# A causal attention loop of sixteen groups, its steps put in another order on every engine

## The reference, cut to what matters

```python
x = x + _L0_xattn_ref(_layernorm(x), ctx, Wq, Wk, Wv, ..., causal mask)
q, k, v = (xn @ W).reshape(B, T, H, hd).transpose(0, 2, 1, 3)
attn = einsum('bhqd,bhkd->bhqk', q, k) * scale
kernels = softmax(...).reshape(B * H, 1, 3, 3)      # one 3x3 kernel for each head, from ctx
attn = conv3x3(where(mask, 0, attn), kernels)       # over (query, key)
p = softmax(where(mask, -inf, attn))
out = einsum('bhqk,bhkd->bhqd', p, v); return out @ proj_W + proj_b
```

## Time and profile before

| | us |
|---|---|
| median of 3 runs | 1688.47 (1685.16 to 1690.96) |
| profiled execution, time | 1679.27 |
| its span | 1677.5 |
| TensorE busy in the span | 1115.9 (67%) |
| VectorE busy | 1040.9 (62%) |
| GpSimd busy | 586.5 (35%) |
| ScalarE busy | 524.2 (31%) |

### The profile page before, as it was taken

One profiled execution on the slowest core, in us unless ns is written; L12 is line 12 of the kernel. 1 busy time (PEld: TensorE's weight loads), 2 busy tenths in 40 slices (PEclk: granted clock), 3 DMA queues, 4 the chain that ended last, 5 costly groups with the idle time before them and its releaser, 6 DMA issues. The chain is left out here.

```text
span 1677.5 us, 25997 instructions
## 1 busy us (share of the span) xinstructions
PE 1115.9 (67%) x9324; PEld 732.0 (44%) x9324; DVE 1040.9 (62%) x2987; ACT 524.2 (31%) x1045; POOL 586.5 (35%) x680
## 2 busy tenths in 40 slices
PE   1466988887838992565555289877857987866520
PEld 0333434443325991565545278633326962322210
DVE  2465676766632344799999646465534436578897
ACT  0123444343413551222222033224513522433310
POOL 7042323223241453111031544311244541166675
PEclk8578989898859995555555589889967988876665
DMA  4910000000013222543341012240001220022232
GB/s 118 335 46 1 1 1 1 1 1 14 4 47 103 69 62 73 140 119 99 98 124 47 32 56 65 71 125 1 13 26 50 74 74 13 1 78 82 84 101 83
DMA packets 74245, 106.19 MB, mean 63 GB/s; under 512 B 11501, under 2 KB 55712, under 8 KB 71616
## 3 DMA queue, kind: packets, MB, share of 16 engines
q1 hardware_dynamic: 59968, 72.16, 15.4%
q0 software_dynamic: 14144, 32.32, 6.3%
HBM read 77.10 MB, written 27.33 MB: 62 GB/s over the span
## 5 line engine op out<-in xcount | busy, mean ns | idle before, releaser
L833 POOL DMA_INDIRECT y_d<-arena,goal x138 | 132.5, 960 | 187.9 <-DVE arena L916 114.1
L1682 DVE CUSTOM_DVE_ANT_0 arena<-ps,far 128x512 f32<-128x512 f32 (+3 forms) x256 | 116.5, 488 | 63.2 <-PE ps L1374 61.9
L2015 POOL DMA_INDIRECT wide<-in_w_ud,arena x128 | 130.1, 1017 | 68.5 <-issue 36.4
L2935 PE MATMUL ps<-wide,arena 78*128 78x32 bf16 x3840 | 109.9, 187 | 50.1 <-ACT wide L3048 41.6
L2935 PEld LDWEIGHTS ps<-wide,arena 78*128 78x128 bf16 x3840 | 109.1, 104 | 56.3 <-ACT wide L3048 45.5
L1012 PEld LDWEIGHTS ps<-arena 128*128 128x128 f32 (+1 forms) x1012 | 123.2, 191 | 4.1
L1012 PE MATMUL ps<-arena 128*128 128x128 f32 (+1 forms) x1012 | 123.6, 274 | 0.0
L1291 POOL TENSOR_SCALAR_AFFINE_SELECT arena<-arena 128x520 f32<-128x520 f32 (+1 forms) x64 | 41.1, 653 | 159.8 <-ACT arena L1557 159.7
L1374 PE MATMUL ps<-fr 32*128 32x256 f32 (+3 forms) x256 | 82.9, 402 | 18.4 <-DVE arena L1682 16.7
L1557 ACT ACTIVATE arena<-ps 128x1024 f32<-128x1024 f32 x80 | 78.4, 1022 | 50.8 <-PE ps L1395 50.8
L1003 PE MATMUL ps<-arena 128*128 128x256 f32 x368 | 89.3, 386 | 1.6 <-DVE arena L892 1.6
(11 more groups left out here) (514 smaller groups left out, 2606.0 us busy)
## 6 DMA issues: line engine op xcount, KB each, us to landing
arena<-low_d SPq DMA_DIRECT2D x32, 780.0 KB
xs_d<-zrow SPq DMA_DIRECT2D x1, 10320.0 KB, 36.0
arena<-xs_d SPq DMA_DIRECT2D x69, 129.0 KB, 2.1
arena<-y_d SPq DMA_DIRECT2D x16, 256.0 KB, 3.2
arena<-in_w SPq DMA_DIRECT2D x2, 1408.0 KB, 9.0
y_d<-arena,goal POOLq DMA_INDIRECT x138, 2.2
wide<-in_Wfc SPq DMA_DIRECT2D x1, 2048.0 KB, 11.5
wide<-in_Wproj SPq DMA_DIRECT2D x8, 256.0 KB, 6.7
```

Source lines behind the costliest of these rows:

```text
L833: pool.indirect_dma_start(out=y_d, in_=yb[:, i % 2, c, :], in_offset=None, out_offset=bass.IndirectOffsetOnAxis(ap=goal[:, i % 4, c:c + 1] ...
L1682: ins = nc.vector.tensor_tensor_reduce(junk[:, n % 2, 384 * i:384 * i + w], ps[:, n % 2, 384 * i:384 * i + w], far[:, T - w:T], 1.0, 3 * N ...
L2015: pool.indirect_dma_start(out=rows_g[t % 4][:, h, :], out_offset=None, in_=A["w_ud"], in_offset=bass.IndirectOffsetOnAxis(ap=eidi[:, t % 8 ...
L2935: mm = nc.tensor.matmul(ps[:, 2 * (i % 3) + h // 2, col:col + 4 * HD], ring[m_ % 4][:, h * NK + p_, t % 2 * P:t % 2 * P + P], table[n // 4 ...
```

## The change

The same instructions are issued with the exception of the join, which is cut in two; what changes is their order.

- **TensorE**: a group begins with `scores(G, 0)`, then `top(0)`. The three query matmuls stand one by one between `top(0)` and `top(3)`. The other steps are dealt out between the tops anew; `weighted(3G+2)` moves from the next group to the end of its own, behind `maximum_rows(G+1)`, and `shifted(.., 2)`, `normed` and the router's turn stand ahead of `maximum_rows`. `projected`, `logits` and `places` stand behind it.
- **VectorE**: `near_scores` of a key group, `near_shift` and the router's `norms` are at the head of the next group; then ten maxima, `outputs`, two maxima, `maximum_out`. `mixed_keys` is cut: its first two passes (`first_mix`) stand between `maximum_out` and `maximum_in`, its third (`last_mix`) behind `maximum_in`. `join` does heads 0 to 11 at the end of the fourth group of an item and heads 12 to 15 at the end of the next group; both stand behind `maximum_in`.
- **ScalarE**: `keys_rounded` is last in a group, `queries` is behind the first exps, `near_exps` ahead of the third.
- **GpSimd**: `products` is behind the third `select`.
- The list of uses of bank 7 follows.

```diff
@@ TensorE
+                        scores(G, 0)
                         top(0)
-                        if G + 2 <= last:
-                            queries(G + 2)
-                        top(1)
-                        scores(G, 0)
-                        top(2)
-                        if G:
-                            weighted(3 * G - 1)
-                        top(3)
+                        for dy in range(3):
+                            if G + 2 <= last:
+                                queries(G + 2, dy, dy + 1)
+                            top(dy + 1)
+
+                        scores(G, 1)
+                        top(4)
+                        weighted(3 * G)
+                        top(5)
                         if G + 2 <= last:
                             keys(G + 2)
...
+                        top(6)
+
+                        scores(G, 2)
+                        top(7)
+                        if nb < B:
+                            shifted(nb, nt, 0)
+                        top(8)
+                        weighted(3 * G + 1)
+                        top(9)
+                        if G:
+                            outputs_turned(G - 1)
+                        top(10)
+                        if nb < B:
+                            shifted(nb, nt, 1)
+                        top(11)
                         if G % 4 == 1 and G >= 5:
                             joined(G // 4 - 1)
...
                         if nb < B:
                             shifted(nb, nt, 2)
                         if G % 4 == 2 and G // 4 + 2 < B:
                             normed(G // 4 + 2)
                         if G % 4 == 3 and G >= 7:
                             R_.turn(pe, take, G // 4 - 1)
+                        if G + 1 <= last:
+                            maximum_rows(G + 1)
+                            weighted(3 * G + 2)
+                        if G % 4 == 1 and G >= 5:
+                            projected(G // 4 - 1)
@@ VectorE
                     for G in range(G4):
+                        nb, nt = near_key(G - 1)
+                        if G and nb < B:
+                            near_scores(nb, nt)
+                        if G % 4 == 3:
+                            near_shift(G // 4)
+                        if G % 4 == 2 and G >= 6:
+                            R_.norms(dve, G // 4 - 1)
                         if G + 1 <= last:
-                            maxima(G + 1, 0, 6)
-                        if G + 2 <= last:
-                            mixed_keys(G + 2)
-                        if G + 1 <= last:
-                            maxima(G + 1, 6, 9)
+                            maxima(G + 1, 0, 10)
                         if G:
                             outputs(G - 1)
                         if G + 1 <= last:
-                            maxima(G + 1, 9, 12)
+                            maxima(G + 1, 10, 12)
                             maximum_out(G + 1)
...
-                        if G % 4 == 0 and G:
-                            join(G // 4 - 1)
+                        if G + 2 <= last:
+                            first_mix(G + 2)
+                        if G + 1 <= last:
+                            maximum_in(G + 1)
+                        if G + 2 <= last:
+                            last_mix(G + 2)
                         if G % 4 == 1 and G >= 5:
                             projected(G // 4 - 1)
...
+                        if G % 4 == 3:
+                            join(G // 4, 0, 3 * H // 4)
+                        if G % 4 == 0 and G:
+                            join(G // 4 - 1, 3 * H // 4, H)
+                        if G % 4 == 0 and G // 4 + 2 < B:
+                            norms(G // 4 + 2)
+                        if G % 4 == 1 and G // 4 + 2 < B:
+                            normed(G // 4 + 2)
+                        if G % 4 == 1 and G >= 9:
+                            R_.pick(dve, ch, G // 4 - 2)
                         if G % 4 == 2 and G >= 6:
                             R_.normed(dve, G // 4 - 1)
...
                     outputs(last)
                     R_.take_logits(dve, ch, arrived, 2)
-                    join(B - 1)
+                    join(B - 1, 3 * H // 4, H)
@@ GpSimd
                         to_experts(1)
+                        to_experts(2)
                         if G % 4 == 2 and G >= 6:
                             R_.rstd_of(pool, ch, G // 4 - 1)
+                        select(3 * G + 2)
+                        to_experts(3)
                         if nb < B:
                             products(nb, nt)
-                        to_experts(2)
-                        select(3 * G + 2)
-                        to_experts(3)
```

More of the change, by code:

```diff
@@ L1203, in first_causal @@
                     plan("q", G + 2); plan("k", G + 2)
-                if G % 4 == 1 and G >= 5:
-                    plan("num", G // 4 - 1)
                 if nb < B:
@@ L1341, in normed, with queries @@
                         mm.then_inc(turn7, 1)
-                    def queries(G):
-                        take("q", G)
-                        pe.wait_ge(free7_act, emptied(place7["ln", G // 4])[0])
-                        for dy in range(3):
+                    def queries(G, lo=0, hi=3):
+                        if lo == 0:
+                            take("q", G)
+                            pe.wait_ge(free7_act, emptied(place7["ln", G // 4])[0])
+                        for dy in range(lo, hi):
                             mm = nc.tensor.matmul(bnk(7), wq_rows[:, G % 4, dy, :], xnp[:, G // 4 % 2, 1 + dy:1 + dy + T],
                                                   start=dy == 0, stop=dy == 2)
-                        mm.then_inc(turn7, 1)
+                        if hi == 3:
+                            mm.then_inc(turn7, 1)
                     def keys(G):
@@ L1462, in _ @@
+                        top(8)
[4 more added lines that the diff above has]
+                        top(10)
+                        if nb < B:
+                            shifted(nb, nt, 1)
+                        top(11)
                         if G % 4 == 1 and G >= 5:
                             joined(G // 4 - 1)
-                        top(6)
-                        if nb < B:
-                            shifted(nb, nt, 0)
@@ L1467, in _ @@
-                        top(7)
-                        weighted(3 * G)
-                        top(8)
-                        if G:
-                            outputs_turned(G - 1)
-                        top(9)
-                        scores(G, 2)
-                        if nb < B:
-                            shifted(nb, nt, 1)
-                        top(10)
-                        weighted(3 * G + 1)
-                        top(11)
                         if nb < B:
                             shifted(nb, nt, 2)
-                        if G % 4 == 1 and G >= 5:
-                            projected(G // 4 - 1)
@@ L1491, in _ @@
                             R_.places(pe, take, G // 4 - 2)
-                        if G + 1 <= last:
-                            maximum_rows(G + 1)
                     weighted(3 * last + 2)
@@ L1597, in _ @@
                         if G + 2 <= last:
+                            queries(G + 2)
+                        exps(G, 1)
+                        if G + 2 <= last:
                             keys(G + 2)
-                        exps(G, 1)
+                        if G % 4 == 3:
+                            near_exps(G // 4)
+                        exps(G, 2)
+                        if nb < B:
+                            shifted(nb, nt, 0)
+                            shifted(nb, nt, 1)
                         if G % 4 == 1 and G >= 5:
@@ L1603, in _ @@
                         if nb < B:
-                            shifted(nb, nt, 0)
-                        if G + 2 <= last:
-                            keys_rounded(G + 2)
-                        exps(G, 2)
-                        if nb < B:
-                            shifted(nb, nt, 1)
                             shifted(nb, nt, 2)
@@ L1646, in mixed_keys, with first_mix @@
                     def mixed_keys(G):
+                        first_mix(G)
+                        last_mix(G)
+                    def first_mix(G):
                         dve.wait_ge(free7_act, emptied(place7["k", G])[0])
@@ L1730, in projected @@
+                        ins = nc.vector.tensor_tensor(four(num), four(num), wide(dn), ALU.mult)
+                        if hi == H:
+                            ins.then_inc(c["num"], 1)
                     def projected(b):
@@ L1781, in _ @@
                             R_.slots(dve, ch, arrived, G // 4 - 2)
-                        if G + 1 <= last:
-                            maximum_in(G + 1)
-                        if nb < B:
-                            near_scores(nb, nt)
+                        if G % 4 == 3:
+                            join(G // 4, 0, 3 * H // 4)
```

(7 more changed lines are left out.)

54 lines of the change are left out of this document (25 added, 29 removed).

## The result

The changed kernel takes 1725.64 us (median of 4 runs, 1723.83 to 1727.17), the kernel before on the same chip 1686.82 (1683.61 to 1690.96): ratio 1.0222, 95% interval 1.0189 to 1.0255. It is 38.8 us slower; 14.2 were forecast, and the range ended at 1717.

A forecast was written before the change was run, and what follows sets the result against it. The loop was taken as paced by TensorE plus its idle time. Full-clock loop +21 us, less about 4 for the clock and 2.5 in the tail, gave +14.2: 1688.5 + 14.2 = 1702.7 us, range 1681 to 1717.

The forecast's parts named there:

- the term for the clock: Loop time lost to TensorE work at 1.2 GHz: 19 us against 23.35 before, so about 4 us given back.
- my third rival: Short gaps around `maximum_rows` put half of all groups at the low clock: another 12 us, 1715; chance 0.18.
- The path at the full clock: Loop of groups 0 to 14 if always at 2.4 GHz: 309 us against 288.1 before, +21.
- The stalls S: Waits of `top(2)` at the head of each group for VectorE's first maxima: 30 us in all.
- The closing chain T and the contention: From `top(11)`'s end to `maximum_in`'s end, 55.4 us over 15 groups; VectorE and GpSimd hindering each other make about 7.
- TensorE's own work W: TensorE's work up to the end of `top(11)`: 15.4 us in an ordinary group, 217 in all.
- H: From the end of `maximum_in` to `scores(G, 0)`: 0.05 us, 1.1 to 1.2 in five groups, 6.5 in all.
- Group 3: Sign in the profile after: this ordinary group of the loop takes 19 to 20 us, not 17.1.
- Group 12: Sign in the profile after: this group, which had a whole join, gets shorter by 3 to 5 us.
- The tail: Behind the last outputs the join is only 4 heads, 2.2 us for 4.75: -2.5 us.
- Slower still: Rival: short gaps in every group bring the low clock to half of all groups, another 12 us, 1715; chance 0.18.
- The spreading works: Rival: the 5 to 6 us idle times in the closing chain and their low-clock stretches go: -12, 1676; chance 0.16.

The follow-up runs named there:

- b_qsplit: The kernel before with only its three query matmuls dealt out behind tops 0, 1 and 2; ratio 1.0264 to the kernel before.
- a_fill: The changed kernel with spare full-width matmuls, their results unread, where TensorE stands idle; ratio 1.0064 to the kernel before.
- a_qblock: The changed kernel with the three query matmuls in one block behind the first top; ratio 1.0087 to the kernel before.
- b_join_gaps: The kernel before with the join dealt out in small steps between the maxima; ratio 1.0069 to the kernel before.

## Why the prediction was wrong

**The step that failed is the term for the clock**: "I take eight stretches with about 4.2 us of work in each and the one at the start as it is, 19 us lost against 23.35". It measured 46.6 us, in fourteen stretches with 6.65 us of work each, the one at the start among them with 11.59 us and not 4.42. Both factors were too low. The number: I let the clock fall only at idle times of 2 to 5 us, though my third rival said that most low stretches of the kernel before belonged to shorter ones; ahead of the 13.70 us in group 13 no idle time was longer than 1.25 us. The length: a stretch can last 13.7 us with TensorE never idle, where I had taken it to end once the work was dense again. That b_qsplit and a_fill move the loss both ways with VectorE's list untouched shows that it follows the order and the make-up of TensorE's work.

**The path at the full clock was right**: 305.5 us against 309, in part by luck, as the terms show (cut in after's trace as the forecast cut them, half of the low-clock work taken off):
- *The stalls S*: the ten waits ahead of the third top come to 27.2 us, forecast 30. Group 4 had 4.84 (forecast 4.9), group 5 4.22 (3.4), group 8 3.82 (4.9), group 10 2.79 (2.9), group 12 none (1.1).
- *The closing chain T and the contention*: T comes to 54.6 us over the loop, forecast 55.4; group 3 takes 3.51 us from the last top to the end of `maximum_in`, forecast 3.15 to 3.65. Each of the two three-operand steps of the mix is slowed where `products` runs, as the lines view over the loop shows (busy us, mean ns, idle before); at 752 ns the 28 of them would take 6.3 us less, and the forecast had some 7:

```profile
L1660 DVE SCALAR_TENSOR_TENSOR arena<-arena,wcol 128x512 f32<-128x512 f32 x14 | 14.2, 1014 | 0.5
...
L1665 DVE SCALAR_TENSOR_TENSOR arena<-arena,wcol 128x512 f32<-128x512 f32 x14 | 13.1, 939 | 0.0
```

- *TensorE's own work W*: one term was missing. The sum took the queries at their price in a block, "two thirds of the queries 1.8"; dealt out they cost 0.5 us more a group, 7 us in all, and the 7.2 us less of a_qblock bear it out. H and W together still come to 223.7 us, forecast 223.5, so other parts of them were as much too high; that this term came out is luck. The forecast's own figures don't add up quite either: 15.4, 13.2 and 9.5 us by group make 218.5 for W and not 217, the parts named for T make 54.6 and not 55.4, and the total is +14.0 and not +14.2.
- *Group 3*: 19.75 us, forecast 19 to 20. *Group 12*: at the full clock 22.49 - 6.4 = 16.1 us against 20.3 before, 4.2 shorter as forecast; the clock leaves 1.1 of it.
- *The tail*: from the end of the last `maximum_in` to the last item's `joined` it took 24.5 us and now takes 23.3, so -1.2, forecast -2.5. The join's own part came as forecast: TensorE's wait for it fell from 5.16 to 2.72 us; the other 1.2 us went ahead of it.

```profile
477.49 1.09 PE L1421 MATMUL ps<-ident,arena 128*128 128x128 f32 x4 [5.16 <-DVE arena L1728]
...
517.31 1.09 PE L1425 MATMUL ps<-ident,arena 128*128 128x128 f32 x4 [2.72 <-DVE arena L1740]
```

**The rivals.** "Slower still" had the mechanism, short gaps that let the clock fall, but at 12 us instead of 28 too cheap, with a chance of 0.18. "The spreading works" was held against the right thing: the third top's waits are there. Of the signs I had named, the idle time in the loop rose by 8.4 us and didn't fall.

**What stays open.** Why the clock stays down for 13.7 us of gapless work in one group and comes back after 3.4 us in another. The length of the wait doesn't say: in after the three longest waits (4.84, 4.22 and 3.82 us) come with 6.83 us at 1.2 GHz each, while a stretch of 10.24 us in group 9 had no idle time over 0.92 us in the 7 us ahead of it:

```profile
358.38:368.62 10.24, 10.24 (x32) 4.17 (x28) 6.98 (x22) 3.49 (x5) 0.64 (x1) 0.50 0.00 1
```

Neither the sum of the idle time (b_join_gaps: 43.5 us idle, 99.6 low; before: 51.4 and 46.7) nor the longest gap orders the kernels of the table. All that can be said is that in these profiles each kernel of the changed order without spare full-width work, and each of the old order with a part moved, has 62 to 159 us at 1.2 GHz. And since the parts don't add up, the 38.8 us can't be dealt out to them: undone one at a time they give back 13.5 thousandths (the query block), 6.6 (the join) and nothing (the mix).

## What to carry to other kernels

In a loop like this one, where TensorE is busy 260 of 311 us and some of it at the low clock, price an order twice: the path at the full clock, and the time lost to work at half the clock, with a wide range for the second. The first came within a few us from rows; the second, 23 us in the kernel before, came out anywhere between 13 and 80 us in these kernels. Try to keep the matmuls with all 128 rows in one block: here the block was worth 12 to 14 us of path and 1.1 to 1.35% of the time in the changed order, and splitting it cost 2.6% in the old one. Where a reordered loop got slower and its clock is down, a few spare full-width matmuls in the idle places show in one run whether the clock is a large part of it.

## What the runs showed of the hardware that was not expected

- TensorE worked at 1.2 GHz for 13.70 us on end with no idle time, and in b_qsplit for 30.7 us with 1.4 us idle. The Trainium skill, "TensorE: Matmul & The Clock Gate", Why this matters for your kernels, advises to keep long idle gaps out from between the matmuls; here gaps of at most 1.25 us preceded a fall, and work without a gap stayed at 1.2 GHz, so by these rows that isn't enough, and the measurement decides.
- Adding 123 spare matmul records (1588 to 1711) took the changed kernel from 1.0222 to 1.0064, some 27 us.
- A query matmul took 1.12 us between two 32-row tops and 0.94 in a block, both at the full clock.
- Ratios of single parts ran from 1.0034 to 1.0309 and didn't add: two parts undone together (1.0134) gave no more than the better one by itself (1.0087).
